# Global keys of a pair of heads in one PSUM bank, and identity products at the head of seven stages

## The chip, the cores and the metric

The kernel runs on one core of one Trainium2 chip. The time is that of one launch in microseconds (us) on the device. The median of three runs of the kernel before is 3248.6 us (3243.54 to 3248.65 us).

## What is computed

A hybrid network of eight layers over X of 4 x 1024 tokens by 256 channels, each layer `x = x + f(layernorm(x))`: attention with a decay over distance, a mixture of eight experts, a retention layer, the experts again, windowed attention, a low-rank FFN, a gated recurrence, and the low-rank FFN again. Windowed attention is the layer that the change touches most (16 heads of 16 channels, 4 batches, so 64 heads):

```
qkv = x @ qkv_w.T ;  q, k = rope(q), rope(k)
mask = (i // 64 == j // 64 | i < 4 | j < 4 | abs(i - j) <= 128) & (j <= i)
attn = softmax(where(mask, q @ k.T * HD ** -0.5, min))
out  = (attn @ v) @ out_w.T
```

So each query sees its window of at most 256 keys and the four global keys 0 to 3. The FFN is `gelu((x @ U1) @ V1 + b1) @ U2 @ V2 + b2`, and each expert `gelu(x @ w1) @ w2` on its 256 best tokens.

## The kernel before, in words

`STAGES = "AMBMCFDF"` names eight stages, s0A to s7F, run one after the other. Each stage (or part of one) is a block with one program for each engine: PE multiplies, DVE and ACT read PSUM and do elementwise work, POOL does small arithmetic and indirect transfers, SP issues the transfers. All engines meet between blocks. Work inside a block is ordered by semaphores written by hand: `x_mm`, `e_ok` and so on count up by one for each item, and `wait_ge(x_mm, START + u + 1)` waits for item u.

**s4C, windowed attention**, has three blocks. `project_rotary` (s4Cp) makes q and k by 512 tokens (a group g, eight in all), splits each number in three bf16 parts (`SplitBlocks`), and writes them to the DRAM tensors `qparts` and `kparts`; for every block of 128 keys, kparts has the four global keys in front (KBLK = 132 columns). `heads_window` (s4Ch) goes through 32 pairs of heads. `project_heads` (s4Co; the same function is s0Ao behind the first attention) divides by the softmax sums and multiplies by the output weights.

In `heads_window`, the program of PE does for each pair p sixteen steps j (block blk = j // 4, head r = j % 2, half n = j % 4 // 2):

- `score` (L2363, L2366): scores of a pair 2.5 pairs ahead, into one of three banks `ps_s`; DVE adds the mask and takes the maximum (L2278). The first 40 scores are made before the loop.
- `hidden` (L2383): the mask of a block, 512 columns into one of NX = 4 banks `ps_x`; `shifted` (L2390): the scores less their maximum on top. ACT takes the exponential into PM (L2307).
- `global_scores` behind steps 3, 7 and 15: the scores of the four global keys. Steps 3 and 7 do one head with 512 columns (L2401), step 15 both heads with 256 columns each (L2405), into rows 0 to 3 of a bank of their own; ACT takes the exponential of 4 x 512 numbers into PG (L2317).
- behind step 5, `global_values` (L2415) of the pair before: four f32 products of 4 rows by 512 columns into the rows 0, 32, 64 and 96 of `ps_v` (`tile_position=(0, 32 * j)`), then `values` (L2426) in the same four places; the other half of `values` behind step 9.
- behind step 11, `turned` (L2378): the maxima of pair p + 2 are transposed, ACT negates them (L2298, L2299), POOL splits them and writes them into rows 96 to 98 of Q (L2253 to L2261).

The four banks are used in turn; `use_of` numbers the uses, twelve for a pair, and `bank_free(u)` makes PE wait until ACT has read use u - 4. SP loads Q and K of a pair with nine transfers (L2213 to L2222), five pairs ahead; the load of pair p + 5 waits for the last use of pair p. Behind it SP stores the result of the pair before with five (L2228, L2230).

**The other places of the change.** `low_rank_ffn` (s5F, s7F): PE waits for the rows of the layer norm, transposes them (L343), makes `ps_p` (L351), and goes on to hidden, down and outs. The expert block (s1Me, s3Me): PE waits until POOL has gathered the first rows of tokens, transposes them (L1311), and multiplies by the weights (L1326, L1340), eight experts. `project_rotary`: PE waits for the layer norm, transposes (L132) and multiplies (L1865). `project_heads`: PE waits until ACT has made `pick` (L2519) and DVE, ACT and POOL have made the split reciprocals (L2528, L2523, L2510), spreads them over the rows (L2563), and multiplies (L2578).

## Time and profile before

| | us |
|---|---|
| median of three runs | 3248.6 |
| profiled execution, its own time | 3250.33 |
| its span, first to last instruction | 3248.6 |
| busy in the span: PE, DVE, ACT, POOL | 2803.9, 1958.3, 1558.0, 1002.2 |
| s4Ch, first load issued to end of the last copy out of PSUM | 2408.0 to 2743.1 |

The profile gives for each stretch of time the granted clock of PE: 1.00 is its level of 2.4 GHz, 0.50 its level of 1.2 GHz. Its mean over the span is 0.914. Where the seven stages that get identity products begin (us from the start of the span, read from the rows in order of time and the table by stretches):

| stage | products | another engine's first instruction | PE's first instruction | clock at PE's first instruction | clock reaches 1.00 |
|---|---|---|---|---|---|
| s0Ao | 8 | 941.16 | 949.76 | 0.50 | 953.7 |
| s1Me | 8 | 1100.81 | 1110.43 | 0.50 | 1117.5 |
| s3Me | 8 | about 1814 | 1823.8 | 0.50 | 1830.9 |
| s4Cp | 5 | 2228.77 | 2233.55 | 0.50 | 2240.5 |
| s4Co | 8 | 2748.34 | 2757.28 | 0.50 | 2762.7 |
| s5F | 5 | 2796.61 | 2801.51 | 0.50, since 2800.3 | 2820.8 |
| s7F | 5 | 3120.26 | 3125.14 | 0.50, since 3121.1 | 3145.0 |

How to read the rows: a row of the list in order of time has the start, the duration from the first to the last instruction of the row, engine, line, operation, what is written and read, and how many instructions; in brackets how long the engine had been idle and who ended it. A row by stretch has the stretch, its length, the busy us (and instructions) of PE, PEld, DVE, ACT and POOL in this order, the granted clock of PE, the busy share of the DMA engines, and GB/s.

### The profile page before, as it was taken

What the parts mean: (1) busy time and instruction counts of PE and PEld (TensorE: products, weight loads), DVE (VectorE), ACT (ScalarE), POOL (GpSimd) and SP (SyncE); (2) the same over time, 40 slices, a digit from 0 to 9 for tenths busy, and PEclk for the clock granted to TensorE, in tenths of its full rate; (3) what the DMA queues carried; (4) which work ended last, traced back from release to release, by engine and by line L of the source; (5) the groups of instructions that cost most, each with busy time, mean ns of one, the idle gap of its engine ahead of it and who ended that gap; (6) DMA issues with size and microseconds to landing.
All of it is one profiled execution on the core that took longest, in us unless ns stands there. A gap on an engine that the chain in (4) does not pass through costs nothing. (4 is left out here: it accounts for less than half of the span.)

```text
span 3248.6 us, 48213 instructions
## 1 busy us (share of the span) xinstructions
PE 2803.9 (86%) x15883; PEld 1690.6 (52%) x15883; DVE 1958.3 (60%) x4266; ACT 1558.0 (48%) x2949; POOL 1002.2 (31%) x1384
## 2 busy tenths in 40 slices
PE   8699999999985399997873599996969997897879
PEld 3244444444442289995551498983534443544443
DVE  7678888888827644443548544444946663527952
ACT  4257777777741245443111345452326665255545
POOL 4322222222201144542001245442654442121112
PEclk9679999999997699998996799997979999898979
DMA  8622222222223144432003244423243432200001
GB/s 291 221 60 67 77 63 81 64 74 71 59 66 130 57 85 92 89 68 65 0 1 130 71 92 85 97 40 88 79 125 95 102 100 63 60 1 0 0 7 46
DMA packets 183367, 248.64 MB, mean 77 GB/s; under 512 B 39512, under 2 KB 128344, under 8 KB 183152
## 3 DMA queue, kind: packets, MB, share of 16 engines
q1 hardware_dynamic: 151376, 210.96, 21.4%
q0 software_dynamic: 30720, 33.98, 6.5%
q8 instruction: 113, 1.85, 0.2%
q10 hardware_dynamic: 1056, 1.02, 0.1%
q14 instruction: 102, 0.84, 0.1%
HBM read 153.39 MB, written 90.90 MB: 75 GB/s over the span
## 5 line engine op out<-in xcount | busy, mean ns | idle before, releaser
L2013 DVE CUSTOM_DVE_ANT_0 s0Ah_SD<-s0Ah_ps_s,s0Ah_table 128x1024 f32<-128x1024 f32 x512 | 607.2, 1222 | 155.1 <-PE s0Ah_ps_s L2071 155.0
L2037 ACT ACTIVATE s0Ah_PM<-s0Ah_ps_x 128x512 f32<-128x512 f32 x1024 | 530.7, 602 | 191.5 <-PE s0Ah_ps_x L2096 100.3
L2071 PE MATMUL s0Ah_ps_s<-s0Ah_plus_k,s0Ah_plus_q 48*128 48x512 f32 x1024 | 424.7, 479 | 25.4 <-DMA s0Ah_plus_k<-s0A_parts 21.6
L1993 POOL TENSOR_TENSOR s0Ah_DG<-s0Ah_SD,s0Ah_mx 128x128 f32<-128x128 f32 x512 | 204.6, 400 | 553.6 <-DVE s0Ah_mx L2013 553.6
L2071 PEld LDWEIGHTS s0Ah_ps_s<-s0Ah_plus_k,s0Ah_plus_q 48*128 48x128 f32 x1024 | 168.1, 194 | 275.1 <-DVE s0Ah_mx L2013 177.7
L2116 PE MATMUL s0Ah_ps_v<-s0Ah_PM,s0A_V 128*17 128x512 f32 x2048 | 273.6, 607 | 0.0
L2096 PE MATMUL s0Ah_ps_x<-s0Ah_plus_q,s0Ah_plus_k 50*128 50x512 f32 (+3 forms) x640 | 238.4, 389 | 0.0
L2278 DVE CUSTOM_DVE_ANT_0 s4Ch_SD<-s4Ch_ps_s,s4Ch_table 128x264 f32<-128x264 f32 x448 | 177.4, 430 | 94.5 <-PE s4Ch_ps_s L2363 90.0
L2096 PE MATMUL s0Ah_ps_x<-s0Ah_minus_q,s0Ah_minus_k 50*128 50x512 f32 (+3 forms) x640 | 219.7, 391 | 0.0
L2307 ACT ACTIVATE s4Ch_PM<-s4Ch_ps_x 128x512 f32<-128x512 f32 (+1 forms) x256 | 131.3, 564 | 114.0 <-PE s4Ch_ps_x L2390 110.7
L2105 PE MATMUL s0Ah_ps_x<-top_ident,s0Ah_DG 128*128 128x128 f32 x512 | 169.6, 331 | 0.0
L1288 ACT ACTIVATE s1Me_hid<-s1Me_ps_h 128x512 f32<-128x512 f32 x128 | 76.5, 598 | 183.2 <-PE s1Me_ps_h L1326 182.8
L1288 ACT ACTIVATE s3Me_hid<-s3Me_ps_h 128x512 f32<-128x512 f32 x128 | 76.5, 598 | 183.2 <-PE s3Me_ps_h L1326 183.2
L1189 POOL DMA_INDIRECT s1M_acc<-s1Me_ys,s1Me_keep x64 | 111.3, 1739 | 163.5 <-DVE s1Me_ys L1253 148.9
L1189 POOL DMA_INDIRECT s3M_acc<-s3Me_ys,s3Me_keep x64 | 109.5, 1711 | 166.4 <-DVE s3Me_ys L1253 151.7
L1243 DVE TENSOR_TENSOR s3Me_HT_rest<-s3Me_hid,s3Me_HT_top 128x512 fp32r<-128x512 f32 x128 | 89.0, 695 | 102.6 <-ACT s3Me_HT_top L1289 99.7
L1243 DVE TENSOR_TENSOR s1Me_HT_rest<-s1Me_hid,s1Me_HT_top 128x512 fp32r<-128x512 f32 x128 | 88.9, 694 | 102.7 <-ACT s1Me_HT_top L1289 98.4
L1340 PE MATMUL s3Me_ps_o<-s3Me_w_top,s3Me_HT_top 128*128 128x256 f32 x512 | 145.0, 283 | 0.0
L1340 PE MATMUL s1Me_ps_o<-s1Me_w_top,s1Me_HT_top 128*128 128x256 f32 x512 | 145.0, 283 | 0.0
L1340 PE MATMUL s1Me_ps_o<-s1Me_w_rest,s1Me_HT_top 128*128 128x256 f32 x512 | 144.0, 281 | 0.0
L1340 PE MATMUL s3Me_ps_o<-s3Me_w_rest,s3Me_HT_top 128*128 128x256 f32 x512 | 144.0, 281 | 0.0
L1340 PE MATMUL s1Me_ps_o<-s1Me_w_top,s1Me_HT_rest 128*128 128x256 f32 x512 | 143.8, 281 | 0.0
(438 smaller groups left out, 6731.7 us busy)
## 6 DMA issues: line engine op xcount, KB each, us to landing
s1W_raw_w<-in_L_ffn_w SPq DMA_DIRECT2D x16, 1024.0 KB
s3W_raw_w<-in_L_ffn_w SPq DMA_DIRECT2D x16, 1024.0 KB
s0A_parts<-s0Ap_sp_top SPq DMA_DIRECT2D x24, 512.0 KB
s0A_parts<-s0Ap_sp_rest SPq DMA_DIRECT2D x24, 512.0 KB
s0Ah_plus_q<-s0A_parts SPq DMA_DIRECT2D x64, 128.0 KB, 2.6
s0Ah_plus_k<-s0A_parts SPq DMA_DIRECT2D x64, 128.0 KB, 3.1
s0Ah_minus_q<-s0A_parts SPq DMA_DIRECT2D x64, 112.0 KB, 2.6
s0Ah_minus_k<-s0A_parts SPq DMA_DIRECT2D x64, 112.0 KB, 2.8
```

The lines of the kernel that those rows point to most:

```text
L1189: pool.indirect_dma_start(out=acc[:, :], out_offset=bass.IndirectOffsetOnAxis(ap=keep[:, BH * v + k // C, k % C:k % C + 1], axis=0), in_=y ...
L1243: nc.vector.tensor_tensor(HT[1][:, m, :], hid[:, m % NH, :], HT[0][:, m, :].bitcast(F32), ALU.subtract).then_inc(h_rest, 1)
L1288: nc.scalar.activation(hid[:, m % NH, :], ps_h[:, m % NH, :], ACT.Gelu_apprx_tanh)
L1340: x = nc.tensor.matmul(ps_o[:, k // 2, (k % 2) * D:(k % 2 + 1) * D], HT[hp][:, m, k * P:(k + 1) * P], w2p[s][wp][:, m, :], start=(m == 0 a ...
L1993: nc.gpsimd.tensor_tensor(DG[p % 3][:, r * TB + t, :], SD[i % NSD][:, t * P:(t + 1) * P], mx[p % 3][:, r * TB + t:r * TB + t + 1].to_broad ...
L2013: nc.vector.tensor_tensor_reduce(SD[i % NSD][:, :], ps_s[i % 2][:, :, :].rearrange("p a n -> p (a n)"), table[:, (TB - 1 - t) * P:(TB - 1 ...
L2037: nc.scalar.activation(PM[n % NPB][:, :], ps_x[u % NX][:, :], ACT.Exp).then_inc(e_ok, 1)
L2071: x = nc.tensor.matmul(ps_s[i % 2][:, half, :], q[at(r), t * P:(t + 1) * P], k[at(r), half * GT:(half + 1) * GT], start=True, stop=True)
L2096: x = nc.tensor.matmul(bank[:, lo:hi], k[with_m(r), t * P:(t + 1) * P], q[with_m(r), half * GT + lo:half * GT + hi], start=True, stop=True)
L2105: nc.tensor.transpose(ps_x[u % NX][:, t % G * P:(t % G + 1) * P], DG[p % 3][:, r * TB + t, :], ident[:, :]).then_inc(x_mm, 1)
L2116: x = nc.tensor.matmul(ps_v[j * 32:j * 32 + HD + 1, :], V[:, n // H, n % H, t, :], PM[w % NPB][:, :], start=(t == 0), stop=(t == TB - 1), ...
L2278: nc.vector.tensor_tensor_reduce(SD[i % NS][:, 0:n], ps_s[i % NS][:, 0:n], mask, 1.0, -3e38, ALU.add, ALU.max, accum_out=mx[p % 3][:, r * ...
```

## The change

1. The four global keys of each batch are written once more behind the blocks of `kparts` (columns 1056 to 1059), loaded with the rest of K, and followed in K by 28 columns of zeros. `global_scores` is called once in a pair, behind step 7: four bf16 products, each with 32 columns of weights, into the rows 0, 32, 64 and 96 of one bank. ACT has two exponentials of 256 columns in place of three of 512, over 128 and 64 rows. A pair has ten uses of the banks.
2. `VG` holds for each pair a matrix of 128 x 128 with the values of the global keys in four blocks. `global_values` is one full f32 product of 512 columns. VG is cleared by POOL and filled by four transfers out of V that SP issues behind the loads of the first five pairs; PE waits for them (`globals_in`) ahead of its loop over the pairs. Cleaning `ps_v` by DVE falls away.
3. The memory clearing of K's rows 96 to 98 by POOL (L2248) comes behind the clearing of PG, the 28 columns and VG. The loads of pair p + 5 wait for the last scores of pair p in place of its last globals. In `SplitBlocks` the writes to k are by c, t, q apart, and POOL has three small copies more in every second group.
4. `keep_dense` puts n products of the identity matrix by itself, 512 columns each, at the head of PE's program in seven blocks, into a bank that is overwritten later.

```diff
+def keep_dense(nc, ident, bank, n):
+    for _ in range(n):
+        nc.tensor.matmul(bank, ident[:, :], ident[:, :].unsqueeze(1).to_broadcast([P, GT // P, P]),
+                         start=True, stop=True)
...
     low_rank_ffn, PE:     +            keep_dense(nc, ident, ps_o[:, :], 5)
     expert block, PE:     +            keep_dense(nc, ident, ps_o[:, 0, :], 8)
     project_rotary, PE:   +            keep_dense(nc, ident, ps_r[:, 0, :], 5)
     project_heads, PE:    +            keep_dense(nc, ident, ps_o[0][:, :, :].rearrange("p a n -> p (a n)"), 8)
...
-            blocks = self.k[n][s][:, :, :].rearrange("p c (t w) -> p c t w", w=KBLK)
-            self.nc.gpsimd.tensor_copy(blocks[:, :, :, 0:NGL],
-                                       self.k[n][0][:, :, NGL:2 * NGL].unsqueeze(2).to_broadcast([P, DC, G, NGL])
-                                       ).then_inc(self.glob, 1)
+            first = self.k[n][0][:, :, NGL:2 * NGL]
+            if s:
+                self.nc.gpsimd.tensor_copy(self.k[n][s][:, :, G * KBLK:], first)
+            self.nc.gpsimd.tensor_copy(self.blocks(n, s)[:, :, :, 0:NGL],
+                                       first.unsqueeze(2).to_broadcast([P, DC, G, NGL])).then_inc(self.glob, 1)
...
-    K = [ph.sb(f"K{i}", [P, 2, TB * KBLK], BF16) for i in range(NST)]
+    KX = TB * KBLK
+    KW = KX + NGL
+    K = [ph.sb(f"K{i}", [P, 2, KX + 32], BF16) for i in range(NST)]
-    PG = [ph.sb(f"PG{i}", [NGL, 2, T]) for i in range(2)]
+    PG = [ph.sb(f"PG{i}", [P, GT]) for i in range(2)]
+    VG = ph.sb("VG", [P, NP, P])
-        return LATE + 12 * p - ...
+        return LATE + 10 * p - ...
...
             for p in range(NST):
                 load(p)
+            sp.wait_ge(clear_ok, START + 3 + NST)
+            for half in range(2):
+                for r in range(2):
+                    at = (2 * half + r) * 32
+                    to = (2 * r + half) * 32
+                    heads = V[0:NGL, :, :, 0, :].rearrange("p b h d -> p (b h) d")
+                    sp.dma_start(VG[at:at + NGL, :, to:to + HD + 1], heads[:, r:B * H:2, :]).then_inc(globals_in, 16)
...
-                nc.gpsimd.memset(PG[i][:, :, :], 0.0).then_inc(clear_ok, 1)
+                nc.gpsimd.memset(PG[i][:, 0:2 * P], 0.0).then_inc(clear_ok, 1)
             for i in range(NST):
-                nc.gpsimd.memset(K[i][96:96 + PARTS, :, :], 1.0).then_inc(ones_ok, 1)
+                nc.gpsimd.memset(K[i][:, :, KW:], 0.0).then_inc(clear_ok, 1)
+            nc.gpsimd.memset(VG[:, :, :], 0.0).then_inc(clear_ok, 1)
+            pool.wait_ge(clear_ok, START + 3 + NST)
+            for i in range(NST):
+                nc.gpsimd.memset(K[i][96:96 + PARTS, :, 0:KW], 1.0).then_inc(ones_ok, 1)
...
+            def global_exps(p):
+                u = global_use(p)
                 act.wait_ge(x_mm, START + u + 1)
+                nc.scalar.activation(PG[p % 2][:, 2 * P:], ps_x[u % NX][:, 2 * P:], ACT.Exp, scale=HD ** -0.5)
+                nc.scalar.activation(PG[p % 2][64:P, 0:2 * P], ps_x[u % NX][64:P, 0:2 * P], ACT.Exp, scale=HD ** -0.5
+                                     ).then_inc(e_ok, 1)
...
+            def global_scores(p):
+                u = global_use(p)
                 q, k = Q[p % NST], K[p % NST]
                 bank_free(u)
+                for half in range(2):
+                    lo = 0 if half else 2 * P
                     for r in range(2):
+                        at = (2 * half + r) * 32
+                        x = nc.tensor.matmul(ps_x[u % NX][at:at + 32, lo:], k[0:99, r, KX:KX + 32],
+                                             q[0:99, r, half * GT + lo:(half + 1) * GT], start=True, stop=True,
+                                             tile_position=(0, at))
                 x.then_inc(x_mm, 1)

             def global_values(p):
                 pe.wait_ge(e_ok, START + last_use(p) + 1)
                 pe.wait_ge(ov_ok, START + p)
-                for half in range(2):
-                    for r in range(2):
-                        j, head = 2 * r + half, 2 * p + r
-                        nc.tensor.matmul(ps_v[j * 32:j * 32 + HD + 1, :], V[0:NGL, head // H, head % H, 0, :],
-                                         PG[p % 2][:, r, half * GT:(half + 1) * GT], start=True, stop=False,
-                                         tile_position=(0, j * 32))
+                nc.tensor.matmul(ps_v[:, :], VG[:, p, :], PG[p % 2][:, :], start=True, stop=False)
...
             pe.wait_ge(hide_ok, START + 1)
-            pe.wait_ge(vz_ok, START + 1)
+            pe.wait_ge(globals_in, 16 * 4)
             for p in range(NP):
...
-                    if j in (3, 7, 15):
-                        global_scores(p, (3, 7, 15).index(j))
+                    if j == 7:
+                        global_scores(p)
```

## Rows read from the trace of the kernel before

**Rows 1.** The page's first part: busy us of each engine.
```profile
PE 2803.9 (86%) x15883; PEld 1690.6 (52%) x15883; DVE 1958.3 (60%) x4266; ACT 1558.0 (48%) x2949; POOL 1002.2 (31%) x1384
```

**Rows 2.** By stretch: 50 us in the middle of s4Ch.
```profile
2500.00:2550.00 50.00, 50.00 (x456) 23.70 (x454) 31.89 (x164) 31.18 (x71) 21.89 (x49) 1.00 0.41 102
```

**Rows 3.** In order of time, SP in s4Ch: one pair's loads and stores, next pair.
```profile
2458.69 0.32 SPq L2213 DMA_DIRECT2D s4Ch_Q<-s4C_qparts  x1
...
2466.14 0.56 SPq L2230 DMA_DIRECT2D s4C_OS<-s4Ch_OE  x1
2468.43 0.32 SPq L2213 DMA_DIRECT2D s4Ch_Q<-s4C_qparts  x1
```

**Rows 4.** In order of time, PE around two calls of global_scores (steps 3, 15).
```profile
2561.10 0.27 PE L2390 MATMUL s4Ch_ps_x<-s4Ch_Q,s4Ch_K 99*128 99x256 bf16 x1
...
2561.30 0.38 PE L2401 MATMUL s4Ch_ps_x<-s4Ch_Q,s4Ch_K 99*4 99x512 bf16 x1
...
2561.61 0.39 PE L2383 MATMUL s4Ch_ps_x<-s4Ch_hide,s4Ch_same 128*128 128x512 bf16 x1
...
2565.31 0.22 PE L2390 MATMUL s4Ch_ps_x<-s4Ch_Q,s4Ch_K 99*128 99x128 bf16 x1
...
2565.46 0.38 PE L2405 MATMUL s4Ch_ps_x<-s4Ch_Q,s4Ch_K 99*4 99x256 bf16 x2
...
2565.78 0.39 PE L2383 MATMUL s4Ch_ps_x<-s4Ch_hide,s4Ch_same 128*128 128x512 bf16 x1
```

**Rows 5.** In order of time, PE behind step 5: global_values, then values.
```profile
2568.32 0.27 PE L2390 MATMUL s4Ch_ps_x<-s4Ch_Q,s4Ch_K 99*128 99x256 bf16 x1
...
2568.52 1.05 PE L2415 MATMUL s4Ch_ps_v<-s4Ch_PG,s4C_V 4*17 4x512 f32 x8
...
2569.50 1.06 PE L2426 MATMUL s4Ch_ps_v<-s4Ch_PM,s4C_V 128*17 128x256 f32 x16
```

**Rows 6.** Groups by line: ACT's exponentials of the global keys, all pairs.
```profile
L2317 ACT ACTIVATE s4Ch_PG<-s4Ch_ps_x 4x512 f32<-4x512 f32 x96 | 54.7, 570 | 0.0
```

**Rows 7.** In order of time, the start of s4Ch: POOL, PE's loop, SP's last early load.
```profile
2410.86 9.05 POOL L2248 MEMSET s4Ch_K<- 3x2112 bf16 x5
...
2423.16 0.42 POOL L2253 TENSOR_TENSOR s4Ch_NR<-s4Ch_NM 16x128 f32<-16x128 f32 x1 [3.24 <-ACT s4Ch_NM L2299]
...
2430.40 0.58 PE L2383 MATMUL s4Ch_ps_x<-s4Ch_hide,s4Ch_same 128*128 128x512 bf16 x1 [0.74 <-DMA s4Ch_Q<-s4Ch_NM]
...
2435.05 0.59 SPq L2222 DMA_DIRECT2D s4Ch_K<-s4C_kparts  x1
```

**Rows 8.** DMA issues: count, KB each, median us from issue to landing.
```profile
s4Ch_K<-s4C_kparts SPq DMA_DIRECT2D x96, 66.0 KB, 2.5
```

**Rows 9.** In order of time, the start of s4Co.
```profile
2748.34 3.27 ACT L2519 CAST s4Co_pick<-top_ident 128x128 fp32r<-128x128 f32 x16 [5.26 <-PEq L62]
...
2757.28 0.76 PE L2563 MATMUL s4Co_ps_b<-s4Co_rc_top,s4Co_pick 128*128 128x512 f32 x1 [14.83 <-POOL s4Co_rc_rest L2510]
...
2760.83 4.34 PE L2578 MATMUL s4Co_ps_o<-s4Co_wo,s4Co_OT 128*128 128x256 f32 x15
```

**Rows 10.** In order of time, PE in s4Cp: two full f32 products of 512 columns each.
```profile
2236.39 3.75 PE L1865 MATMUL s4Cp_ps_q<-s4Cp_hT,s3W_raw_w 128*128 128x512 f32 x4 [0.88 <-ACT s4Cp_hT L140]
...
2241.94 1.88 PE L1865 MATMUL s4Cp_ps_q<-s4Cp_hT,s3W_raw_w 128*128 128x512 f32 x4
```

**Rows 11.** In order of time, PE's first work in s1Me and in s5F.
```profile
1110.43 1.97 PE L1311 MATMUL s1Me_ps_t<-top_ident,s1Me_xg 128*128 128x128 f32 x8 [11.85 <-DMA s1Me_xg<-s1M_h_rows,s1Me_cols]
...
2805.07 3.78 PE L351 MATMUL s5F_ps_p<-s5F_hT,s4Cw_u 128*128 128x512 f32 x4 [0.67 <-ACT s5F_hT L298]
```

**Rows 12.** By stretch: a rise of the clock in s4Co, a fall in s2B.
```profile
2761.00:2763.00 2.00, 2.00 (x7) 1.61 (x6) 0.69 (x1) 0.00 (x0) 0.00 (x0) 0.57 0.74 206
...
1566.00:1567.00 1.00, 0.00 (x0) 0.00 (x0) 1.00 (x4) 0.00 (x0) 0.00 (x0) 1.00 0.00 0
...
1568.00:1569.00 1.00, 1.00 (x5) 0.90 (x4) 0.00 (x0) 1.00 (x2) 0.00 (x0) 0.53 0.00 0
```

More of the change, by code:

```diff
@@ L384, in outs @@
                 x.then_inc(o_mm, 1)
+            keep_dense(nc, ident, ps_o[:, :], 5)
             pe.wait_ge(W.weights, W.loaded)
@@ L1699, in __init__ @@
         self.q = [[ph.sb(f"sp_q{n}{s}", [P, DC, GT], BF16) for s in range(2)] for n in range(PARTS)]
-        self.k = [[ph.sb(f"sp_k{n}{s}", [P, DC, G * KBLK], BF16) for s in range(2)] for n in range(PARTS)]
+        self.k = [[ph.sb(f"sp_k{n}{s}", [P, DC, G * KBLK + NGL], BF16) for s in range(2)] for n in range(PARTS)]
         self.f_ok = ph.sem("sp_f")
@@ L1707, in out, with blocks @@
         if which == 0:
-            return self.q[n][s][:, :, :].rearrange("p c (t q) -> p (c t) q", q=P)
-        return self.k[n][s][:, :, :].rearrange("p c (t w) -> p (c t) w", w=KBLK)[:, :, NGL:]
+            return self.q[n][s][:, :, :].rearrange("p c (t q) -> p c t q", q=P)
+        return self.blocks(n, s)[:, :, :, NGL:]
+    def blocks(self, n, s):
+        return self.k[n][s][:, :, 0:G * KBLK].rearrange("p c (t w) -> p c t w", w=KBLK)
     def tiles(self, t, s, which):
-        return t[s][:, which, :, :].rearrange("p c (t q) -> p (c t) q", q=P)
+        return t[s][:, which, :, :].rearrange("p c (t q) -> p c t q", q=P)
     def scalar_first(self, act, g):
@@ L1852, in _ @@
         def _(pe):
+            keep_dense(nc, ident, ps_r[:, 0, :], 5)
             ln.tensor(pe, 0)
@@ L2178, in heads_window, with global_use @@
     s_mm, m_ok, x_mm, e_ok = ph.sem("s_mm"), ph.sem("m_ok"), ph.sem("x_mm"), ph.sem("e_ok")
-    nr_ok, pv_mm, ov_ok, vz_ok = ph.sem("nr_ok"), ph.sem("pv_mm"), ph.sem("ov_ok"), ph.sem("vz_ok")
+    nr_ok, pv_mm, ov_ok = ph.sem("nr_ok"), ph.sem("pv_mm"), ph.sem("ov_ok")
     N = NP * U
-    MAXIMA = 8
+    MAXIMA, GLOBALS = 7, 4
     def use_of(p, k):
-        return LATE + 12 * p - max(p - (NP - LATE), 0) + k - (k > MAXIMA and p >= NP - LATE)
+        return LATE + 10 * p - max(p - (NP - LATE), 0) + k - (k > MAXIMA and p >= NP - LATE)
     def score_use(p, r, block):
-        return use_of(p, 3 * block + r)
-    def global_use(p, n):
-        return use_of(p, (2, 5, 11)[n])
+        return use_of(p, (0, 2, 5, 8)[block] + r)
+    def global_use(p):
+        return use_of(p, GLOBALS)
     def turn_use(p):
@@ L2197, in last_use @@
     def last_use(p):
-        return global_use(p, 2)
+        return score_use(p, 1, 3)
     LOADS = 9 * 16
@@ L2215, in load @@
                 sp.dma_start(q[5 * HD:6 * HD, :, :], both(qparts[rows, 0, :])).then_inc(done, 16)
-                sp.dma_start(k[5 * HD:6 * HD, :, :], both(kparts[rows, 2, :])).then_inc(done, 16)
+                sp.dma_start(k[5 * HD:6 * HD, :, 0:KW], both(kparts[rows, 2, :])).then_inc(done, 16)
                 for r in range(2):
                     one = slice((2 * p + r) * HD, (2 * p + r + 1) * HD)
-                    sp.dma_start(k[0:3 * HD, r, :], kparts[one, 0:1, :].to_broadcast([HD, 3, TB * KBLK])
+                    sp.dma_start(k[0:3 * HD, r, 0:KW], kparts[one, 0:1, :].to_broadcast([HD, 3, KW])
                                  ).then_inc(done, 16)
                     sp.dma_start(q[3 * HD:5 * HD, r, :], qparts[one, 0:2, :]).then_inc(done, 16)
-                    sp.dma_start(k[3 * HD:5 * HD, r, :], kparts[one, 1:2, :].to_broadcast([HD, 2, TB * KBLK])
+                    sp.dma_start(k[3 * HD:5 * HD, r, 0:KW], kparts[one, 1:2, :].to_broadcast([HD, 2, KW])
                                  ).then_inc(done, 16)
@@ L2308, in exps @@
                                      ).then_inc(e_ok, 1)
-            def global_exps(p, n):
-                u = global_use(p, n)
+            def global_exps(p):
+                u = global_use(p)
                 act.wait_ge(x_mm, START + u + 1)
-                if n < 2:
-                    to, at = PG[p % 2][:, n, 2 * P:6 * P], ps_x[u % NX][0:NGL, :]
-                else:
-                    to, at = PG[p % 2][:, :, 6 * P:], ps_x[u % NX][0:NGL, :].rearrange("p (r q) -> p r q", r=2)
-                nc.scalar.activation(to, at, ACT.Exp, scale=HD ** -0.5).then_inc(e_ok, 1)
+                nc.scalar.activation(PG[p % 2][:, 2 * P:], ps_x[u % NX][:, 2 * P:], ACT.Exp, scale=HD ** -0.5)
+                nc.scalar.activation(PG[p % 2][64:P, 0:2 * P], ps_x[u % NX][64:P, 0:2 * P], ACT.Exp, scale=HD ** -0.5
+                                     ).then_inc(e_ok, 1)
             def collect(p):
@@ L2341, in _ @@
                         exps(p, r, blk)
-                    if blk < 2:
-                        global_exps(p, blk)
+                    if blk == 1:
+                        global_exps(p)
                     if blk == 2:
@@ L2394, in shifted @@
                     x.then_inc(x_mm, 1)
-            def global_scores(p, n):
-                u = global_use(p, n)
+            def global_scores(p):
+                u = global_use(p)
                 q, k = Q[p % NST], K[p % NST]
                 bank_free(u)
-                if n < 2:
-                    x = nc.tensor.matmul(ps_x[u % NX][0:NGL, :], k[0:99, n, NGL:2 * NGL], q[0:99, n, 2 * P:6 * P],
-                                         start=True, stop=True)
-                else:
+                for half in range(2):
+                    lo = 0 if half else 2 * P
                     for r in range(2):
-                        x = nc.tensor.matmul(ps_x[u % NX][0:NGL, 2 * r * P:2 * (r + 1) * P],
-                                             k[0:99, r, NGL:2 * NGL], q[0:99, r, 6 * P:], start=True, stop=True)
+                        at = (2 * half + r) * 32
+                        x = nc.tensor.matmul(ps_x[u % NX][at:at + 32, lo:], k[0:99, r, KX:KX + 32],
+                                             q[0:99, r, half * GT + lo:(half + 1) * GT], start=True, stop=True,
+                                             tile_position=(0, at))
                 x.then_inc(x_mm, 1)
```

17 lines of the change are left out of this document (9 added, 8 removed).

## The prediction

> **What bounds the kernel now.** I read the page's totals first [rows 1]: PE is busy 86% of the span, the next engine 60%. That is a mean over eight stages, so I went on to the stage that the first three edits touch. In s4Ch the table by stretches has PE busy in all of 50 us, while DVE has 31.9, ACT 31.2 and POOL 21.9 [rows 2]: PE sets the pace at its 2.4 GHz level. The list in order of time then gives the period of a pair: the first load of one pair is issued at 2458.69 and of the next at 2468.43, which is 9.74 us, and SP itself is through with its fourteen transfers at 2466.70, 8.01 us after it began [rows 3]. So time comes out of this stage only by shortening PE's stream, and SP is the next bound at 8.0 us, 1.7 us below.
>
> For the identity products the reader needs two things from the same list: how long PE stands still at the head of a block, and at which clock it then starts. The table in the section on the profile has both. In five of the seven places PE idles 5 to 10 us, then does its first 3 to 7 us of work at 1.2 GHz; in s5F and s7F it stays at 1.2 GHz for 19 us, because it waits often.
>
> **Part 1, the two calls of global_scores that fall away.** At step 3, `shifted` starts at 2561.10 and streams 256 columns, and the next `hidden` starts at 2561.61: 0.51 us. The 256 columns need 0.11 (L2390 and its neighbours start 0.11 apart), so the call costs 0.40 [rows 4]. At step 15 it is 2565.31 to 2565.78, 0.47, less 0.06 for 128 columns: 0.41. About half of either is no streaming: there is a gap ahead of the small product and one behind it. Two calls in each of 32 pairs: 2 x 0.40 x 32 = 25.6 us off PE.
>
> **Part 2, the call that stays, behind step 7.** It costs 0.40 too. In the new form four products go to four column places. Do they overlap? The old global_values is the nearest row: four f32 products of 512 columns, each in its own column place, take from 2568.52 to 2569.50, 0.98 us [rows 5], and one full f32 product of 512 columns takes 0.86 (four records, so two products, start at 2241.94 and the next group at 2243.65) [rows 10]. Four took the time of about one. So I take 512 bf16 columns once (0.21) and at worst the 256 columns before them (0.11), and the same two gaps of 0.1: 0.41 to 0.52, mean 0.46. Cost 0.06 a pair, 1.9 us. Lower bound -0.05 a pair; upper bound, if none overlap, 1536 columns are 0.64 and the gaps 0.2, so +0.44 a pair, 14 us.
>
> **Part 3, global_values as one full product.** Before: 2568.32 to 2569.50 with `shifted` ahead, 1.18 us [rows 5]. After: 0.11 + 0.86 + a gap ahead of `values`, 0.1, and perhaps 0.1 for 128 columns of f32 weights: 1.07 to 1.18. I count it as nothing, with -0.1 a pair as the far end. The Trainium skill says that a change of tiling mode drains the engine (TensorEngine Tiling (Array Packing), Key Properties). The gaps around the small products in rows 4 agree with it; by the rule, the one product takes away no change of mode, it only moves it behind itself.
>
> **Part 4, ACT, DVE, banks and SP.** ACT loses three exponentials of 0.57 us [rows 6] and gets two of 256 columns. It had 31.2 of 50 us, so this is hidden by PE and worth nothing, except at the end: the last globals stand on the path to the last values, 0.6 us. With ten uses, PE's waits for banks change little; I went through the uses and found only waits of under 0.1 us that exist today. SP's loads and stores take 8.0 us of a period that falls to about 9.0, so they stay hidden. If the period fell below 8.0, SP would take over.
>
> **Part 5, the new wait ahead of PE's loop.** Today the loop starts at 2430.40. SP issues the ninth transfer of the fifth pair at 2435.05 and is free at 2435.7 [rows 7]. Only then come the four transfers for VG. One issue takes 0.5 to 0.6 us, so the last is out at 2438.0, and one lands 2.5 us behind its issue at the median [rows 8]: 2440.5. Behind the waiting instruction on PE stand the masks, scores and everything else of pair 0; DVE has had its 40 scores and waits, and ACT too. All of it slips: 10.1 us. The other uses of VG would have had time: the first global_values comes 11.5 us behind the start of the loop. Bounds: 8 us (fast issues, 2 us to land) and 13 us (many pieces of 68 bytes, slow to land). POOL's order changes as well. Clearing 2112 elements takes 1.8 us [rows 7], so VG's 4096 take 3.5, the rest about 1, and K's rows 96 to 98 are ready at about 2421.5, ahead of 2423.16 when POOL is needed: hidden, by 1.6 us. POOL's extra copies in s4Cp: 0.3 us at the tail of that block.
>
> Stage s4Ch with s4Cp's tail: -25.6 + 1.9 - 0.6 + 10.1 + 0.3 = **-13.9 us**.
>
> **Part 6, the identity products.** One costs 0.86 us at 2.4 GHz and 1.78 at 1.2 (2236.39 to 2239.94 for two) [rows 10]. PE begins them when the block opens. The clock rose 5.4 us after PE began to work without gaps in s4Co [rows 9, 12] and 3.9 in s0Ao; I take 4.7, in which 2.6 products pass.
> - s4Co: eight products from 2748.3 are done at 2753.0 + 5.4 x 0.86 = 2757.6, 0.3 late. The spreading then runs at twice the pace, DVE has its first two tiles at about 2760.1 and L2578 begins 0.7 earlier than at 2760.83; what followed until 2762.7 at 1.2 GHz took 1.0 too much. -1.7 us. PE is the bound behind it (busy in all of the stretch), so this lasts. s0Ao: done at 950.5, 0.75 late, -0.6.
> - s1Me: from 1100.8, done at 1110.1, before 1110.43 [rows 11]. The transposes come out 0.85 earlier. Behind them PE idles over 2 us; if the clock holds, 1.5 more is won up to 1117.5. s2B has a case near: a gap of 2.1 us, and the clock had fallen a microsecond behind it [rows 12]. Half and half: -1.6 each, -3.2 for both expert stages.
> - s4Cp: done at 2235.5, 2 us behind 2233.55, then twice as fast until 2240.5: +0.9 and -2.05, -1.15.
> - s5F: the block opens at 2796.5, 1.4 us behind PE's last work and with the clock still up, so five products take 4.3 and are done at 2800.8, before 2801.5. L351 falls from 3.6 to 1.7 us [rows 11], each pair of transposes by 0.5. PE works under half of the time until 2812, so I expect the clock to fall again on the way: -3 (bounds -2 and -5.5). s7F opens 1.8 us behind PE's last work, at 3120.3, and the clock fell at 3121.1: products partly at 1.2 GHz, -1 (bounds +1 and -4).
>
> Sum -10.7 us, bounds -4 and -18. The Trainium skill states that transposes do not count as work for the clock (TensorE: Matmul & The Clock Gate, Part 4). That speaks against lasting gains where transposes come next, as in s1Me, s3Me, s5F and s7F. If all four lost their extra, the sum would be about -8; the case in s2B points the same way but had a gap too.
>
> **Sum.** -13.9 - 10.7 = -24.6 us. Against the profiled execution that is 3250.3 - 24.6 = 3225.7; it stood 1.7 above the median of the runs, so I give 3224.
>
> **Rivals.**
> - *The four column products do not overlap.* Against: rows 5. For: these have 32 columns of weights each and are bf16, with little streaming to hide the loads. Then +14 in place of +1.9: 3236. Chance 0.12.
> - *The wait is longer or the products give nothing, so that most is eaten.* The clock falls behind every set of products and only s4Co, s0Ao and s4Cp keep their 3.5 us, while the head of s4Ch costs 13: 3234 to 3240. Chance 0.13.
> - *No change to be measured* (within 0.2%, 6.5 us, about what a measurement of this kernel can tell from none): the stall grows to 20 us or more because VG's small pieces land slowly, and the gain of the loop is halved. Chance 0.07.
> - *Slower.* Identity products, nearly all zeros, do not raise the clock. Then eight take 14.2 us and five 8.9: PE starts late by 5.7 (s0Ao), 5.3, 4.6, 4.6, 4.1 and about 1, 25 us against the -13.9 of s4Ch: +11, 3260. It decides from 14 us on. Against: dense f32 products of that size are what raised the clock in s4Co. Chance 0.06.
> - *More is won.* The clock holds in s5F, s7F and the experts (-18), and the waits for banks shrink as well: 3212. Chance 0.14.
> The rest, 0.48, is the forecast, itself 3218 to 3231. The range 3210 to 3241 leaves out the two cases above it (0.13) and the far side of "more is won" (about 0.05). Faster by over 0.2%: 0.86; within: 0.08; slower: 0.06.
>
> **What would show it.** In the changed profile: the period of SP's loads in s4Ch 9.74 to 9.0 us; one small group of four products 0.4 to 0.5 us long; PE idle ahead of its first row of `hidden`, which starts near 2440 (less what was won before) and whose releaser is the transfer into VG; PE records of identity products at the head of seven blocks, the clock reaching 1.00 inside the sets of eight. The prediction is wrong if the small products start 0.1 to 0.2 us apart, if the transfer of VG lands early or very late, or if the clock stays at 0.50 through the products.

## The result, and the profile after

The changed kernel takes 3228.1 us (median of six runs, 3221.0 to 3233.2), the kernel before 3248.6 beside it (3243.5 to 3255.6): ratio 0.9932, 95% interval 0.9918 to 0.9946, so 18 to 27 us less. Taken again on another chip the ratio was 0.9914 (0.9895 to 0.9933). Forecast were 3224 and a range of 3210 to 3241.

The page's totals, against [rows 1]:

```profile
span 3231.0 us, 47958 instructions
...
PE 2816.2 (87%) x15738; PEld 1704.0 (53%) x15785; DVE 1946.9 (60%) x4265; ACT 1535.6 (48%) x2917; POOL 1005.1 (31%) x1402
```

They tell little: PE has 12 us more work, and this profile's span is 17.6 us shorter. So I measured each stage in the trace, from the first instruction of any engine in it to the first of the next stage, in two profiles of either kernel (the second ones are runs of the experiments below):

| stage | before | after | change | predicted |
|---|---|---|---|---|
| s0Ao | 47.2, 47.9 | 46.8, 47.1 | -0.6 | -0.6 |
| s1Me | 401.1, 401.4 | 400.6, 400.5 | -0.7 | -1.6 |
| s3Me | 401.2, 401.3 | 400.4, 400.4 | -0.8 | -1.6 |
| s4Cp | 178.5, 178.5 | 179.3, 178.8 | +0.6 | -0.85 |
| s4Ch | 341.1, 341.1 | 326.6, 326.8 | -14.4 | -14.2 |
| s4Co | 48.3, 48.2 | 46.5, 46.7 | -1.7 | -1.7 |
| s5F | 124.6, 124.6 | 121.6, 121.0 | -3.3 | -3 |
| s6D | 199.1, 199.0 | 201.6, 202.2 | **+2.9** | 0 |
| s7F | 128.3, 128.4 | 126.2, 126.2 | -2.2 | -1 |
| the rest without s0Ah | 559.5, 560.2 | 559.8, 559.9 | 0 | 0 |
| sum | | | **-20.2** | -24.6 |

s0Ah stands apart. No edit touches it, and it took 819.1 and 815.0 us before, 821.0 and 817.0 after, and 809.8 to 819.4 in the experiments. Its time goes with the clock. PE's clock is at 0.50 from about 110 us on, and the later it comes back to 1.00, the longer the stage: 56 to 57 us behind the start of s0Ah in the two profiles with 809.8 and 810.6 us, 67 to 69 in three with 814.6 to 815.6, 72 to 73 in five with 816.9 to 817.5, 77 to 78 in two with 819.1 and 819.4, and 82.5 in the one with 821.0. That is 0.43 us of time for each us of delay. The six timed runs of the changed kernel fall in two groups with it: 3221.0 to 3224.1 us at a mean granted clock of 0.924 to 0.925, and 3232.1 to 3233.2 at 0.921 to 0.922. So below I compare stages, or the span without s0Ah (2429.5 and 2431.4 before, 2410.0 and 2410.4 after), where a few us decide.

**The loop of s4Ch.** In order of time, SP's first load of two pairs that follow one another, which answer to [rows 3]:

```profile
2449.71 0.32 SPq L2233 DMA_DIRECT2D s4Ch_Q<-s4C_qparts  x1
2458.72 0.31 SPq L2233 DMA_DIRECT2D s4Ch_Q<-s4C_qparts  x1
```

The period is 9.01 us, from 9.74. In order of time, PE around the call that stays, at step 15 where a call is gone, and around global_values (answers to [rows 4, 5]):

```profile
2544.37 0.27 PE L2416 MATMUL s4Ch_ps_x<-s4Ch_Q,s4Ch_K 99*128 99x256 bf16 x1
2544.57 0.40 PE L2431 MATMUL s4Ch_ps_x<-s4Ch_Q,s4Ch_K 99*32 99x256 bf16 x4
2544.90 0.39 PE L2409 MATMUL s4Ch_ps_x<-s4Ch_hide,s4Ch_same 128*128 128x512 bf16 x1
...
2548.61 0.22 PE L2416 MATMUL s4Ch_ps_x<-s4Ch_Q,s4Ch_K 99*128 99x128 bf16 x1
2548.66 0.38 PE L2409 MATMUL s4Ch_ps_x<-s4Ch_hide,s4Ch_same 128*128 128x512 bf16 x1
...
2550.97 0.27 PE L2416 MATMUL s4Ch_ps_x<-s4Ch_Q,s4Ch_K 99*128 99x256 bf16 x1
2551.09 1.02 PE L2439 MATMUL s4Ch_ps_v<-s4Ch_PG,s4Ch_VG 128*128 128x512 f32 x2
2552.04 1.06 PE L2448 MATMUL s4Ch_ps_v<-s4Ch_PM,s4C_V 128*17 128x256 f32 x16
```

The four column products cost 2544.90 - 2544.37 - 0.11 = 0.42 us, 0.02 more than the old call; at step 15 `hidden` follows `shifted` after 0.05 where it took 0.47; global_values takes 1.07 where it took 1.18. By these three places a pair should be 0.91 us shorter (0.40 + 0.42 + 0.11 - 0.02), and it is 0.73. Where the other 0.18 went shows in the distances from the start of one `shifted` (L2390, now L2416) to that of the next, 16 in a pair, as means of pairs 6 to 25 of either profile:

| behind step | before, us | after, us |
|---|---|---|
| 1 and 2, together | 0.454 | 0.612 |
| 3 (a call is gone) | 0.855 | 0.447 |
| 5 (global_values) | 2.296 | 2.178 |
| 7 (the call that stays) | 0.799 | 0.820 |
| 15 (a call is gone) | 0.805 | 0.420 |
| the ten others, together | 4.535 | 4.537 |
| the pair | 9.744 | 9.014 |

So 0.16 us a pair is lost behind steps 1 and 2. There a `score` waits for DVE: it needs a bank of `ps_s` whose maximum DVE has taken. In order of time, the loading of weights of the score ahead of step 3, and from the table of waits, 2500 to 2590 us (in all, times, longest); the same table of the kernel before has no such row:

```profile
2549.95 0.10 PEld L2389 LDWEIGHTS s4Ch_ps_s<-s4Ch_K,s4Ch_Q 96*128 96x128 bf16 x1 [0.24 <-DVE s4Ch_mx L2308]
```

```profile
PEld s4Ch_ps_s L2389 <- DVE s4Ch_mx L2308: 4.3, 20, 0.2
```

DVE takes 0.35 us for a maximum there and works without a pause from 2548.40 on, so with the calls gone PE reaches it. By stretch, the middle of the stage (answers to [rows 2]; columns as there):

```profile
2500.00:2550.00 50.00, 49.29 (x456) 26.35 (x464) 32.87 (x181) 30.85 (x75) 21.73 (x48) 1.00 0.42 103
```

The 0.71 us that PE lacks here are not idle time: this trace has the multiplication of only 209 of the 256 calls of `hidden`, though the weights of all 256, and each of its eight gaps in this stretch lies where such a record is missing. The distances between the starts do not depend on that.

**The head of s4Ch.** In order of time, SP's transfers for VG, PE's last scores ahead of the loop, the loading of weights for its first `hidden`, and the first score in the loop (answers to [rows 7]):

```profile
2428.77 1.72 PE L2389 MATMUL s4Ch_ps_s<-s4Ch_K,s4Ch_Q 96*128 96x264 bf16 x5
...
2435.93 2.86 SPq L2259 DMA_DIRECT2D s4Ch_VG<-s4C_V  x4
...
2441.05 0.10 PEld L2409 LDWEIGHTS s4Ch_ps_x<-s4Ch_hide,s4Ch_same 128*128 128x128 bf16 x1 [10.86 <-issue]
...
2441.45 0.43 PE L2389 MATMUL s4Ch_ps_s<-s4Ch_K,s4Ch_Q 96*128 96x264 bf16 x1 [10.97 <-DMA s4Ch_VG<-s4C_V]
```

The bracket is the forecast's part 5: what released PE was the transfer into VG. The multiplication of the first `hidden` is one of the missing records, so PE stood for about 10.6 us (2430.49 to 2441.05) and not 10.97. From SP's first load of the stage the loop's first score starts after 32.1 us, before after 22.75: 9.4 us later, forecast 10.1.

**The identity products.** In order of time, the head of s4Co (against [rows 9]), and by stretch, one microsecond on either side of the clock's rise:

```profile
2735.24 9.61 PE L164 MATMUL s4Co_ps_o<-top_ident 128*128 128x512 f32 x16 [5.55 <-PEq L62]
2744.29 0.80 PE L2586 MATMUL s4Co_ps_b<-s4Co_rc_top,s4Co_pick 128*128 128x512 f32 x1
...
2746.76 3.50 PE L2601 MATMUL s4Co_ps_o<-s4Co_wo,s4Co_OT 128*128 128x256 f32 x15
```

```profile
2739.00:2740.00 1.00, 1.00 (x2) 0.46 (x2) 1.00 (x1) 0.00 (x0) 0.00 (x0) 0.50 0.22 71
2741.00:2742.00 1.00, 1.00 (x3) 0.40 (x3) 1.00 (x1) 0.00 (x0) 0.00 (x0) 1.00 0.83 230
```

The clock rose inside the set, 5.1 us behind its first product. The spreading L2586 starts 9.05 us into the stage, where it was 8.94, and L2601 only 2.47 us later instead of 3.55.

The expert stages kept little of it. In order of time, the head of s1Me (against [rows 11]), and two stretches:

```profile
1109.81 1.02 PE L164 MATMUL s1Me_ps_o<-top_ident 128*128 128x512 f32 x2
1111.96 1.10 PE L1320 MATMUL s1Me_ps_t<-top_ident,s1Me_xg 128*128 128x128 f32 x8 [1.13 <-DMA s1Me_xg<-s1M_h_rows,s1Me_cols]
1115.10 0.47 PE L1335 MATMUL s1Me_ps_h<-s1Me_xT_top,s1Me_w_top 128*128 128x512 f32 x1 [2.05 <-issue]
...
1116.12 0.63 PE L1335 MATMUL s1Me_ps_h<-s1Me_xT_top,s1Me_w_top 128*128 128x512 f32 x1
```

```profile
1110.00:1111.00 1.00, 0.83 (x2) 0.00 (x1) 0.00 (x0) 0.00 (x0) 0.69 (x2) 1.00 1.03 406
1117.00:1118.00 1.00, 1.00 (x4) 0.81 (x3) 0.50 (x1) 0.72 (x2) 0.55 (x1) 0.50 0.00 0
```

The clock was at its upper level when the products ended at 1110.83. PE then stood 1.1 us ahead of the transposes and 2.05 us behind them, and the clock had fallen when its real work began: L1335 takes 0.63 us there, as before, and not 0.39.

### The profile page after: what moved, and what is told of

Read it like the earlier page. It is cut to its first block and busy times, and to the rows that moved or that the text cites. A ratio compares the mean times of both kernels' runs of the same rounds, so it can differ in the third digit from the quotient of the medians.

```text
span 3231.0 us, 47958 instructions
## 1 busy us (share of the span) xinstructions
PE 2816.2 (87%) x15738; PEld 1704.0 (53%) x15785; DVE 1946.9 (60%) x4265; ACT 1535.6 (48%) x2917; POOL 1005.1 (31%) x1402
## 3 DMA queue, kind: packets, MB, share of 16 engines
q10 hardware_dynamic: 1056, 1.02, 0.1%
## 5 line engine op out<-in xcount | busy, mean ns | idle before, releaser
L2088 PEld LDWEIGHTS s0Ah_ps_s<-s0Ah_plus_k,s0Ah_plus_q 48*128 48x128 f32 x1024 | 168.6, 195 | 276.0 <-DVE s0Ah_mx L2030 178.5
L2308 DVE CUSTOM_DVE_ANT_0 s4Ch_SD<-s4Ch_ps_s,s4Ch_table 128x264 f32<-128x264 f32 x448 | 168.2, 429 | 92.2 <-PE s4Ch_ps_s L2389 89.7
```

What stands on the lines that cost most here:

```text
L2088: x = nc.tensor.matmul(ps_s[i % 2][:, half, :], q[at(r), t * P:(t + 1) * P], k[at(r), half * GT:(half + 1) * GT], start=True, stop=True)
L2308: nc.vector.tensor_tensor_reduce(SD[i % NS][:, 0:n], ps_s[i % NS][:, 0:n], mask, 1.0, -3e38, ALU.add, ALU.max, accum_out=mx[p % 3][:, r * ...
```

## Experiments

Each was timed beside the kernel before on the same chip; the one with a single place, the one with transposes and the repeated kernel before ran once each, for their profile. VG means the block matrix of the globals' values.

### The wait for VG where it is needed

```diff
             def global_values(p):
                 pe.wait_ge(ov_ok, START + p)
+                pe.wait_ge(globals_in, 16 * 4)
...
-            pe.wait_ge(globals_in, 16 * 4)
             for p in range(NP):
```

> The changed kernel with PE's wait for VG moved from in front of its loop to just ahead of the first product that reads VG (inside the call of global_values for pair 0). Theory A: the 11.0 us in which PE stood for that wait come back, less the 1.3 us in which PE would have waited for the rows of Q anyway; the loop starts some 9.8 us earlier and the time falls from 3228.1 to about 3218 us. VG lands at about 2441 and is first read 11.5 us behind the start of the loop, at about 2443, so it is not waited for. Rival B: the wait only moves: the four transfers of VG sit in SP's queue ahead of the loads of the sixth pair, or VG lands behind its first use, and 2 us or more of it are paid again: 3220 to 3226.

Measured: 3218.5 us (3206.1 to 3221.5), ratio 0.9905 (0.9889 to 0.9922); s4Ch 316.5 us. In order of time, the first score of the loop, the transfers and the first product that reads VG:

```profile
2418.41 0.42 PE L2389 MATMUL s4Ch_ps_s<-s4Ch_K,s4Ch_Q 96*128 96x264 bf16 x1 [0.63 <-DVE s4Ch_mx L2308]
...
2423.27 2.86 SPq L2259 DMA_DIRECT2D s4Ch_VG<-s4C_V  x4
...
2428.97 1.02 PE L2440 MATMUL s4Ch_ps_v<-s4Ch_PG,s4Ch_VG 128*128 128x512 f32 x2
```

The product carries no bracket: nothing was waited for. Theory A holds, to 0.3 us in the stage (-10.1 against -9.8). The change as made pays 10 us for the place of one wait. The ratios alone would not give that size: 0.9905 here against 0.9932 and 0.9914 for the change as made.

### The global edits alone, the products alone

The one is the changed kernel without its four calls of keep_dense, the other the kernel before with them.

> The changed kernel without any identity product; the three edits on the global keys stay. By the stages of the two profiles the edits in s4Ch and s4Cp are worth -14.5 + 0.8 = -13.7 us against the kernel before: about 3235 us, so the products would be worth 7 us. Rival: the 2.5 us that s6D lost behind s5F belong to the products, and their net worth is only 4 to 5 us: about 3232.

> The kernel before with the identity products alone. By the stages of the two profiles: s0Ao -0.4, s1Me -0.5, s3Me -0.8, s4Cp 0, s4Co -1.8, s5F -3.0, s7F -2.2, sum -8.7: about 3240 us if s6D keeps its time, 3242.4 if s6D loses 2.5 again. The prediction's sum was -10.7: 3238.

Measured: without products 3240.2 us, ratio 0.9971 (0.9962 to 0.9979), s4Ch 326.7 and s4Cp 179.2. Products alone 3238.2, ratio 0.9969 (0.9958 to 0.9981), s0Ao 46.3, s1Me 400.6, s3Me 400.4, s4Cp 178.0, s4Co 46.2, s5F 122.5, s7F 126.9. So each half is worth some 9 to 10 us in time. The 3235 us expected without products, and the rival's 3232, were both too low; the products alone came in below the 3240 to 3242 expected. In stages s4Ch keeps its -14.4 with no product anywhere. The products' stages gain -0.5 to -2.1, not all as they did together: s5F -2.1 where it was -3.3, s7F -1.5 where it was -2.2, s0Ao -1.3 where it was -0.6. But **s6D is 202.4 us in the one and 202.1 in the other**: it is slower with either half, and no edit of either touches it. That is 3 of the 5 us by which the edits on the globals were timed under their stages (-14.4 + 0.75 in stages, -8.6 in time), and it was not forecast.

### s6D, the kernel before once more

> The kernel before, profiled once more. In its first profile s6D took 199.1 us, in those of the changed kernel and of three variants 201.4 to 202.4, one of them without identity products. If that is scatter, a second profile of the same kernel has s6D at up to 202 us; if the edits on the globals cause it, it has 199.1 again.

Measured: 3248.2 us, s6D 199.04. So it is not mere scatter, and it is not the edits on the globals alone, since the products by themselves do it too. By stretch, 7 us of s6D's head and 3 us behind them, first in this profile of the kernel before, then (next fence) at the same distance from the stage's start in that of the kernel with the global edits, the late wait and no products (told below), whose s6D took 202.5:

```profile
2924.00:2931.00 7.00, 4.52 (x17) 3.66 (x18) 2.88 (x12) 2.33 (x5) 1.21 (x2) 0.50 0.00 0
2931.20:2934.20 3.00, 3.00 (x9) 1.32 (x8) 0.49 (x1) 0.78 (x4) 0.00 (x0) 1.00 0.00 0
```

```profile
2902.40:2909.40 7.00, 4.57 (x18) 3.66 (x19) 2.84 (x12) 2.38 (x6) 1.21 (x2) 0.50 0.01 2
2909.60:2912.60 3.00, 3.00 (x4) 1.12 (x4) 0.00 (x0) 0.56 (x3) 0.00 (x0) 0.50 0.00 0
```

The work is the same (4.52 and 4.57 us of PE), and the clock rises 12.2 us behind the start of s6D in the one and 15.5 in the other. In all eleven profiles without products in s6D a later rise goes with a longer stage: rise at 12.2 (twice, both of the kernel before) 199.1 and 199.0 us; at 13.9 200.9; at 14.4 and 14.5 (twice) 201.4 to 201.6; at 15.0 202.1; at 15.2 (twice) to 15.5 202.2 to 202.5. But the first rise is less than half of it. Followed by the starts of DVE's instructions, the changed kernel is 1.1 us behind the kernel before at 24 us into the stage, 2.2 at 83 and 2.9 at 127: the rest is lost in later stretches at 0.50, which lie elsewhere too. In all, the clock is at 0.50 for 58.0 us of s6D in both profiles of the kernel before, and for 64.9 to 65.7 in the nine others.

s2B, the retention layer, untouched as well, shows that it is this whole pattern that counts and not the first rise. It took 199.6 to 199.8 us with a rise at 18.1 to 18.4 us (five profiles) and 200.1 to 200.2 with one at 18.9 to 19.0 (four); but with one at 15.8 to 16.5, which is earlier, it took 200.4 to 200.9 (four); there the clock fell once more at 43 to 44 us. What the edits change for s6D is the moment of its start and the clock's state ahead of it. That this alone shifts the pattern is argued and not shown: no run moves the start of s6D and leaves the rest as it is.

### Do four column places overlap?

```diff
-                        x = nc.tensor.matmul(ps_x[u % NX][at:at + 32, lo:], k[0:99, r, KX:KX + 32],
+                        x = nc.tensor.matmul(ps_x[u % NX][0:32, lo:], k[0:99, r, KX:KX + 32],
...
-                                             tile_position=(0, at))
+                                             tile_position=(0, 0))
```

> The changed kernel with all four products of a call of global_scores in one and the same column place (they overwrite each other, so what the exponentials read is not the globals' scores), to see whether four places overlap at all. If they overlap as the old global_values did, the period of a pair grows from 9.01 us by about 0.3 (the 1536 columns in a row take 0.64 and not some 0.3), to about 9.3, and the span by 10 us. If they did not overlap, the period stays 9.01.

Measured: s4Ch 340.5 us against 326.6, 13.9 us or 0.43 a pair. In order of time, the group of four, here and (second fence) in the changed kernel's next pair:

```profile
2555.96 0.82 PE L2431 MATMUL s4Ch_ps_x<-s4Ch_Q,s4Ch_K 99*32 99x256 bf16 x4
```

```profile
2553.59 0.40 PE L2431 MATMUL s4Ch_ps_x<-s4Ch_Q,s4Ch_K 99*32 99x256 bf16 x4
```

They overlap: 1536 columns in a row are 0.64 us (the forecast's part 2), and the group takes 0.40. Expected for one place were 0.3 us a pair and 10 us; measured are 0.43 and 14. One after the other they cost the 14 us that the forecast gave as its upper bound, and s4Ch would then be only 0.6 us shorter than before, the stall included.

### Products across the gap in the expert stages

```diff
-            keep_dense(nc, ident, ps_o[:, 0, :], 8)
+            keep_dense(nc, ident, ps_o[:, 0, :], 9)
             transposes(0, 0, 0)
+            keep_dense(nc, ident, ps_o[:, 0, :], 2)
             expert_turns(pe, turn)
```

> The version with the late wait for VG, and in the two expert stages nine identity products in place of eight ahead of the first transposes and two more behind them, in the 2.05 us in which PE stands before its first L1335. Theory A: the clock, which rose in the products and fell again at 1115.55, because PE had stood 1.1 and 2.0 us around the transposes, stays at 1.00; the eight or so products at 1.2 GHz become fast and each expert stage shortens by 1.3 to 2 us: 3 us in all, 3215.5. Rival B: transposes keep the clock from counting as busy or ACT and DVE set the start of the first turn, so that nothing is won: 3218.5.

Measured: 3206.7 us (3206.3 to 3210.5), ratio 0.9862 (0.9843 to 0.9881). Stages: s1Me 399.8, s3Me 399.2, against 400.4 to 400.6 in the two profiles of the changed kernel. The medians, 11.8 us below the late wait alone, say nothing of the bridge's size: the two profiled spans are 3.4 us apart, with s3Me 1.1 shorter and s1Me 0.7 longer, and s4Cp, s6D, s2B and s0Ao, which this edit does not touch, 0.6 to 1.4 shorter. In order of time, and by stretch:

```profile
1101.14 1.04 PE L1320 MATMUL s1Me_ps_t<-top_ident,s1Me_xg 128*128 128x128 f32 x8
1102.01 1.88 PE L164 MATMUL s1Me_ps_o<-top_ident 128*128 128x512 f32 x4
1104.22 0.47 PE L1335 MATMUL s1Me_ps_h<-s1Me_xT_top,s1Me_w_top 128*128 128x512 f32 x1 [0.33 <-issue]
1104.53 0.40 PE L1335 MATMUL s1Me_ps_h<-s1Me_xT_rest,s1Me_w_top 128*128 128x512 f32 x1
```

```profile
1105.00:1106.00 1.00, 1.00 (x6) 0.82 (x5) 1.00 (x2) 0.98 (x2) 0.55 (x1) 1.00 0.00 0
```

The clock held, and L1335 ran at 0.40 us from its second product on, though it began 0.8 us later in the stage. So theory A in kind; in size 0.7 and 1.2 us, not 1.3 to 2. One thing limits it: of the twelve expert stages in the six profiles with eight products and no bridge the clock fell in ten (400.3 to 400.7 us) and held in two, both s1Me, where it had risen late, 5.2 and 6.0 us in (398.9 and 399.1); the set then lasted 9.7 and 10.1 us in place of 8.7 to 9.1 and left no gap ahead of the transposes. So the 2 us behind them alone are not always fatal, and a fall costs about 1.5 us in s1Me.

### Transposes instead of products

```diff
-    for _ in range(n):
-        nc.tensor.matmul(bank, ident[:, :], ident[:, :].unsqueeze(1).to_broadcast([P, GT // P, P]), ...)
+    for k in range(7 * n):
+        nc.tensor.transpose(bank[:, k % 4 * P:(k % 4 + 1) * P], ident[:, :], ident[:, :])
```

> The version with the late wait for VG, each identity product replaced by seven transposes of the identity, of 128 columns each, so of about the same length. If transposes do not count as work for the clock, it does not rise inside the sets: in s4Co and s0Ao it would rise only some 5 us behind the first L2586, as before the change, and the stages would take 48.3 and 47.4 us again (a little more, since the transposes run at 1.2 GHz and take longer than the wait that they fill). If they count, it rises 3 to 6 us behind the first of them and the stages take 46.5 and 46.6.

Measured: s4Co 46.3 and s0Ao 45.8 us. In order of time the set in s4Co, and by stretch, one microsecond on either side of the rise:

```profile
2720.62 9.27 PE L164 MATMUL s4Co_ps_o<-top_ident 128*128 128x128 f32 x56 [5.55 <-PEq L62]
```

```profile
2724.00:2725.00 1.00, 1.00 (x7) 1.00 (x6) 0.66 (x1) 0.00 (x0) 0.00 (x0) 0.50 0.27 78
2727.00:2728.00 1.00, 1.00 (x12) 1.00 (x11) 0.69 (x1) 0.27 (x1) 0.00 (x0) 1.00 0.86 264
```

The rise came inside the set, 6.1 us behind the first transpose (5.1 with products); in s0Ao 3.9. Transposes of f32 tiles of 128 columns do count for the clock here. The forecast had weighed the opposite statement of the Trainium skill (TensorE: Matmul & The Clock Gate, Part 4), which would have made its sum about -8; the measurement decides against it for this form. One stage did worse: s3Me took 403.6 us, with the clock down from 10.0 to 20.2 us into the stage.

### Products at the head of the gated stage

```diff
+            keep_dense(nc, ident, ps_f[:, 0, :], 4)
             ln.tensor(pe, 0)
+            keep_dense(nc, ident, ps_f[:, 0, :], 2)
             ln.tensor(pe, 1)
```

> The version with the late wait for VG, and at the head of s2B and s6D four identity products ahead of the first transposes and two between the first and the second set. PE stands 5 us there and then works at 1.2 GHz for 7 to 17 us. Theory A: the clock is up by the first product with weights; 1 to 3 us are won in each stage, 3215. Rival B: the first products are late by up to 1 us and the stage is bound by DVE and ACT, so that nothing is won: 3218 to 3220.

Measured: 3214.7 us (3210.7 to 3219.0), ratio 0.9887 (0.9865 to 0.9909). In order of time, PE's first rows in s6D, and (second fence) in s2B:

```profile
2885.31 5.37 PE L164 MATMUL s6D_ps_f<-top_ident 128*128 128x512 f32 x8 [2.02 <-SPq L67]
2890.51 1.04 PE L132 MATMUL s6D_ps_t<-top_ident,s6D_ln_h 128*128 128x128 f32 x8
2891.39 1.88 PE L164 MATMUL s6D_ps_f<-top_ident 128*128 128x512 f32 x4
```

```profile
1502.22 1.94 PE L132 MATMUL s2B_ps_t<-top_ident,s2B_ln_h 128*128 128x128 f32 x8 [19.27 <-DVE s2B_ln_h L115]
```

s6D is 198.7 instead of 200.9 to 202.5, with the clock up 4.9 us into the stage: 2 to 4 us won against the variants without products there, 0.4 against the kernel before. So theory A holds for s6D. For s2B the run says nothing, against what its expectation and that of the next one assume. The edit stands in `gated_recurrence`, which only s6D runs; s2B is the retention layer, its rows have no identity product, and its first work of PE, 7.4 us in, waits for the layer norm and not for weights. Its 200.4 us lie within the scatter of the untouched stage.

### The edits together, and what the products are worth beside the late wait

> The version with the late wait and the bridged expert stages, with four and two identity products at the head of s6D as well (not of s2B, whose weights come 7.4 us into the stage), and seven instead of eight in s0Ao and s4Co. By the stages: s6D 198.7 in place of 201 to 202, the projections 0.2 shorter each at best. Expected -2.5 us against the version with the bridge, so about 3207 to 3214 us, by where the scatter of s0Ah (810 to 821 us in the profiles so far) puts it. Rival: the clock's moments shift in s6D and s7F and what is won in one stage is lost in the next.

> The three edits on the global keys with the late wait and no identity product. Stage s4Ch 316.5 us against 341.1 before, all other stages as before: 24.6 - 0.8 = 23.8 us less than before by the stages, 3225. The difference to the version with late wait and products (3218.5) is the products' worth once more: by the stages 9.5, so rather 3228. Rival: the run without products and with the early wait was timed at only 8.6 us less than before where its stages say 12 to 14; if something outside the profiled stages eats 4 us, this one is at 3230 or more.

> The changed kernel once more, on the chip of the others, so that they stand beside it: 3228 us, s4Ch 326.6 and the expert stages 400.5 each; s0Ah between 810 and 821.

Measured: all together 3212.7 us (3209.7 to 3214.9), ratio 0.9891 (0.9871 to 0.9910), s6D 197.9, s1Me 399.0, s3Me 399.3. Its interval overlaps those of the version with the bridge and of the late wait alone; the span without s0Ah puts them in order: 2398.5 with the late wait, 2394.3 with the bridge, 2390.4 with all, and 2410.0 and 2410.4 for the change as made. So all together lies 3.9 us below the bridge there, where 2.5 was expected; the medians say the opposite, with s0Ah 7 us longer in this profile (817.5 against 810.6). The global edits with the late wait and no products 3227.6 us, ratio 0.9931 (0.9914 to 0.9947), s4Ch 316.8, s6D 202.5: the rival's 3230 was not reached. The products beside the late wait are worth 9.1 us by the medians, taken on two chips whose intervals overlap (3227.6 to 3218.5), and 10.4 by the span without s0Ah (2408.9 to 2398.5). s5F and s7F kept their time with all together (121.1 and 126.4), so the rival that it is lost in the next stage did not come. The change as made on this chip: 3221.8 (3219.6 to 3229.2) where 3228 was expected, with s4Ch 326.8 and the expert stages 400.5 and 400.4 as expected.

## Why the prediction was right, point by point

- **Parts 1 and 2, the calls.** Right: 0.40 and 0.42 us for the calls that fall away, +0.02 for the one that stays (forecast +0.06). The reading from the four old column products carried, and the run with one place showed that it had to: the rival "do not overlap" would have cost just its +14.
- **Part 3.** The far end, -0.1 a pair, is what was measured (-0.11), not the nothing that I took. That the gaps around the small products of [rows 4] come from a change of tiling mode is not shown: `turned`, a product with 16 columns of weights behind step 11, has none: in the kernel before it starts 0.11 us behind `shifted` (2437.17, 2437.28), and `hidden` 0.11 behind it (2437.39). No run takes the gaps apart.
- **Period.** Forecast about 9.0, measured 9.01. Part of this is luck: 0.16 us a pair went to the waits for DVE's maxima behind steps 1 and 2. The prediction had DVE hidden, by its 31.9 of 50 us, but that is a mean over the pair; at the head of a pair DVE has no pause. Part 3 gave back 0.11.
- **Part 5.** Right in place, releaser and size (9.4 us later than before, and 10.1 given back by the late wait, for 10.1). The tail of s4Cp was 0.75 us longer and not 0.3 (179.2 without products against 178.5): the three small copies cost what was forecast (POOL's last copy ended 174.3 us into the stage and not 174.0), but the last of the widened writes landed 3.5 to 3.6 us behind its issue, where it was 2.9.
- **Part 6.** The clock rises in every set that begins at the lower level, 3.1 to 6.1 us in (both profiles), for 4.7 assumed. s4Co, s0Ao and s5F came to the forecast within 0.3 us. Mis-sized were s1Me and s3Me (-0.7 and -0.8 for -1.6 each: of "half and half" mostly the half without the clock came true), s4Cp (-0.5 with products alone and next to nothing beside the global edits, for -1.15: the forecast stopped at PE, but POOL and the last write end that block; with products POOL's last copy ended 174.0 in place of 174.3 us into the stage, but the last write landed at 178.3 and 177.8 us in the two profiles, against 178.2 without products) and s7F (-2.2 for -1: its clock was up through the whole set and 2.9 us on). That s5F came out is in part luck: the clock was to fall again on the way, and it stayed up until 16.6 us; with products alone it fell 7.8 us in, and the stage gained 2.1.
- **What was in no term.** s6D, +2.9 us. The sum treated every stage without an edit as fixed, and one whose clock rises and falls on the way is not.

So -20.2 for -24.6: s6D +2.9, the expert stages +1.7 and s4Cp +1.4 on the one side, s7F, s5F and s4Ch -1.7 on the other. The profiled spans fell by 18.3 us in the mean of two, the 20.2 less the 1.9 us that s0Ah was longer; that the medians fell by 20.5, so near the stages' sum, is luck, as s0Ah's time goes with its clock.

## What to carry to other kernels

A wait belongs in front of the first instruction that needs the data, not in front of the loop that contains it; here that line was worth half the whole gain again, and it could be read beforehand from SP's queue and the landing time. Dense dummy work at the head of a block pays where PE would idle anyway and real PE-bound work follows without a gap; where a gap follows, it has to reach across. And when a change is small beside the launch, compare stage by stage in two profiles of each kernel, with the clock of each stage beside its time: one untouched stage moved by 3 us here and another by 11, both with their clock. Last, the mean busy share hides a bound inside a period: the distances from step to step found the wait for DVE, and they hold where records are missing.
